# A recommendation tower in blocks of 512 samples: wider lookups, gathers that stand still for the grams, and grams turned straight from PSUM

## The chip, the cores and the metric

The kernel runs on one core of a Trainium2 chip. The time is the device time in microseconds (us) of that core; lower is better. The engines are TensorE (PE in the rows, its weight loads PEld), VectorE (DVE), ScalarE (ACT), GpSimd (POOL) and SyncE (SP), which issues DMAs. Each runs its own instruction stream in order, and they wait for each other by semaphores. One changed kernel is compared with one kernel before.

## The reference: what is computed

For each of 2048 samples there is a dense row of 128 numbers and 26 table ids. Each id picks one row of 128 numbers from its table (tables have 1000 to 125000 rows). The 27 vectors are multiplied with each other, and the upper triangle of products goes, with the dense row, into a small network:

```python
e = jnp.stack([tbl_0[ids[:, 0]], ..., tbl_25[ids[:, 25]]], axis=1)      # (2048, 26, 128)
combined = jnp.concatenate([dense_features[:, None, :], e], axis=1)     # (2048, 27, 128)
interactions = jnp.einsum('bfd,bgd->bfg', combined, combined)
iu, ju = jnp.triu_indices(27, k=1)
z = jnp.concatenate([dense_features, interactions[:, iu, ju]], axis=1)  # 128 + 351
h = jnp.concatenate([z, dense_features], axis=1)                        # 607
h = jnp.maximum(h @ W_top1 + b_top1, 0.0)                               # 512
h = jnp.maximum(h @ W_top2 + b_top2, 0.0)                               # 256
y = h @ W_top3                                                          # (2048, 1)
```

All data are fp32.

## The kernel before, in words

The batch is cut into 16 tiles of 128 samples and 8 blocks of 256. `emb` holds, for two blocks, the 27 vectors of each sample with the 128 numbers across the partitions. It is filled in two ways.

A **look** (`look`, L421 and L422) fetches rows of a table of 1000 rows without a gather. The table lies in SBUF as 8 chunks of 128 rows, each split into a high and a low part (`table_hl`). For a chunk c VectorE compares the ids of the block with the row numbers and writes a one-hot matrix `hot` of 128 x 256 (L646; some are made by ScalarE, L529 and L532). PE multiplies the high and the low part of the chunk with it. 8 chunks, 16 matmuls of 256 columns, add up in PSUM, and ScalarE copies two looks at once into `emb` (L538). Ten tables are looked up in the first six blocks and eleven in the last two. `hot` is a ring of 8: VectorE waits for `hot_used`, which PE raises once for each chunk.

An **embed** (`embed`, L432) handles the other tables. GpSimd gathers 128 rows of one table by an indirect DMA (L391). Three or four such rows blocks, one of them the dense rows of the tile, form a group, and a group fills one of 7 slots of `rows`. PE turns the group by transposes, and ScalarE copies it into `emb`. GpSimd waits for `embeds_done` before it uses a slot again, and for nothing else.

The **gram** of a tile is 128 small products, 26 x 26 each. An fp32 product is two MATMUL records in the trace, so a tile has 256 of them, and they are issued in four bursts of 64, with other work of PE between the bursts (L448). ScalarE copies each half tile to `gram_sb` (L563), VectorE transposes 32 x 32 pieces of that into `turned` (L660), and ScalarE picks the 351 products of a sample into `pairs` (L574 to L581). These are ten small copies for each tile.

The **network** runs on units of two tiles (the last two tiles each alone): `z` transposes the pairs, `l1` is 12 matmuls for each of 4 outputs, `l2` is 12 for each of 2 outputs, `l3` is the last layer. ScalarE and VectorE split each result into a high and a low part.

The order is written by a table of times: each step gets a number from `AT` and formulas around it, and all steps, sorted by it, are the list `STEPS`. Each engine runs its share of `STEPS` in that order. GpSimd alone has its own plain loop over tiles and groups.

Of the kernel before, what the change touches and what calls it, by code (L numbers as in the profile page):

```python
# [7 lines left out]
AT = {"high": 0.1, "low": 0.0, "wload": -0.626, "hots": 0.001, "g0": 0.053, "g1": 0.352, "gs": 0.159,  # L8
# [12 lines left out]
BLOCK_LOOKUPS = [10] * 6 + [11] * 2  # L21
# [8 lines left out]
BLOCK = 256  # L30
# [22 lines left out]
def dlrm_tower(nc, dense, ids_gathered, ids_looked_up, tables, w1_dense, w1_pairs, b1, w2, b2, w3, out):  # L53
# [9 lines left out]
    UNIT_OF = {t + i: u for u, (t, n) in enumerate(UNITS) for i in range(n)}  # L63

# [4 lines left out]
    GROUP = [grouped(list(range(BLOCK_LOOKUPS[t * TILE // BLOCK], FEATURES))) for t in range(TILES)]  # L69
# [6 lines left out]
    BURSTS = 2  # L76
# [7 lines left out]
    ACT_CHUNKS = (3, 7)  # L84
# [7 lines left out]

    def look_time(k, h):
        b, i = LOOKS[k]
        return b - 1 + (i + h / 2) / BLOCK_LOOKUPS[b] + (AT["look"] if b else 0.0)

    def embed_time(t, e):
        return ((AT["e0"], AT["e1"], AT["e2"], AT["e3"])[t] if t < 4 else t / 2 + AT["em"]) + AT["es"] * e / len(GROUP[t]) + (AT["em1"] if t % 2 else 0.0) + (
            AT["em14"] if t == TILES - 2 else AT["em15"] if t == TILES - 1 else 0.0)

    for i in range(LOOKUPS):
        at(-1.6 + 0.1 * i if i >= RAW else -2.0 + i / 100, "load", i)
        at(-1.1 + 0.1 * i - AT["high"] if i >= 2 else -1.5 + i / 100, "high", i)
        at(-1.1 + 0.1 * i + AT["low"] if i >= 2 else -1.35 + 0.05 * i, "low", i)
# [6 lines left out]
    for t in range(TILES):  # L111
# [5 lines left out]
        if t >= TILES - 2:  # L117
            begin = t // 2 + (AT["ug1"] if t % 2 else AT["ug0"])
# [609 lines left out]
```

## Time and profile before

| | |
|---|---|
| three runs | 577.74, 588.22, 592.58 us; median 588.22 |
| span of the profiled execution | 590.3 us |
| PE busy | 437.2 us, 6480 matmuls |
| VectorE, ScalarE, GpSimd busy | 256.1, 200.2, 245.8 us |
| granted TensorE clock, mean | 0.820 |

The profiled execution has no time of its own beside its span of 590.3 us; that lies within the three runs, 0.4% above their median. Busy times overlap and say only how long an engine had something in it. A matmul's record lasts longer than the step from one matmul to the next, since matmuls are pipelined: 256 columns last 0.28 us in the record and follow each other after 0.12 us at the full clock.

### The profile page before, as it was taken

Reading aid. Unit: us, or ns where it says so; the run is one execution under the profiler, and the core shown is the slowest. Engines: PE = TensorE matmul, PEld = TensorE weight load, DVE = VectorE, ACT = ScalarE, POOL = GpSimd, SP = SyncE. Lnnn points to the kernel's source line nnn. Section 1 sums busy time; section 2 is a strip of 40 time slices with the busy share of each in tenths; the row PEclk is TensorE's granted clock in tenths of the full one; section 3 lists DMA queues with packets and bytes.
Section 4 is the critical chain, followed back from the end, with each engine's and each line's share of the span. In section 5 each row is a group of like instructions: output and inputs, shape, how many; then the busy total and the mean of one; then the engine's idle time right before and its main releaser. Section 6 shows DMA issues by size and latency. Waiting matters only on the chain.

```text
span 590.3 us, 15061 instructions
## 1 busy us (share of the span) xinstructions
PE 437.2 (74%) x6480; PEld 394.1 (67%) x6480; DVE 256.1 (43%) x745; ACT 200.2 (34%) x497; POOL 245.8 (42%) x261
## 2 busy tenths in 40 slices
PE   5468266967686866977679594795856879769988
PEld 5267155857576755867558593694755868669987
DVE  4278245742235422455324462352531465537321
ACT  3179122432133311333213341142320333225663
POOL 7705664364425443164431655417344254541000
PEclk9569669977799587888778886787676988879999
DMA  7535211111112111021110211102111111111000
GB/s 264 177 113 162 53 48 45 38 54 37 47 33 55 49 39 41 20 59 42 42 41 25 59 42 48 40 25 62 37 42 44 30 53 43 53 44 29 2 4 1
DMA packets 25781, 31.59 MB, mean 54 GB/s; under 512 B 6469, under 2 KB 19669, under 8 KB 25716
## 3 DMA queue, kind: packets, MB, share of 16 engines
q0 software_dynamic: 8064, 16.53, 9.9%
q1 hardware_dynamic: 17620, 14.10, 8.0%
q8 instruction: 51, 0.84, 0.6%
q14 instruction: 14, 0.11, 0.1%
q10 hardware_dynamic: 32, 0.01, 0.0%
HBM read 30.61 MB, written 0.01 MB: 52 GB/s over the span
## 4 chain that ended last, share of the span: by engine, by line
PE 69%; issue 21%; ACT 5%; another core or an unknown queue 4%; DVE 1%; DVEq 0%; ACTq 0%
PE emb_ps L421 17%; PE emb_ps L422 15%; PE mix_ps L448 13%; PE emb_ps L432 6%; PE mlp_ps L479 4%; PE mlp_ps L480 3%; PE mlp_ps L481 3%; ACT emb L538 2%; PE mlp_ps L490 2%; PE mlp_ps L491 2%; PE mlp_ps L492 2%; PE mlp_ps L509 1%; PE mlp_ps L461 1%; ACT table_hl L516 1%
## 5 line engine op out<-in xcount | busy, mean ns | idle before, releaser
L391 POOL DMA_INDIRECT rows<-table,gather_ids x252 | 244.6, 971 | 298.1 <-PE emb_ps L432 218.4
L646 DVE TENSOR_SCALAR hot<-lids,row_number 128x256 fp32r<-128x256 int16 x638 | 198.7, 365 | 237.0 <-PE emb_ps L422 192.3
L421 PE MATMUL emb_ps<-hot,table_hl 128*128 128x256 f32 x656 | 206.4, 340 | 37.4 <-issue 21.3
L422 PE MATMUL emb_ps<-hot,table_hl 128*128 128x256 f32 x656 | 191.7, 317 | 1.9 <-issue 1.9
L421 PEld LDWEIGHTS emb_ps<-hot,table_hl 128*128 128x128 f32 x656 | 147.2, 224 | 49.2 <-issue 27.9
L422 PEld LDWEIGHTS emb_ps<-hot,table_hl 128*128 128x128 f32 x656 | 149.0, 227 | 2.0 <-issue 2.0
L448 PE MATMUL mix_ps<-emb 128*26 128x26 f32 x4096 | 80.1, 196 | 81.6 <-issue 77.2
L538 ACT ACTIVATE emb<-emb_ps 128x512 f32<-128x512 f32 (+1 forms) x118 | 80.8, 689 | 166.1 <-PE emb_ps L432 59.5
L448 PEld LDWEIGHTS mix_ps<-emb 128*26 128x26 f32 x4096 | 58.3, 108 | 106.9 <-issue 96.3
L432 PE MATMUL emb_ps<-ident,rows 128*128 128x128 f32 x268 | 51.7, 319 | 20.6 <-ACT emb L538 11.7
L563 ACT ACTIVATE gram_sb<-mix_ps 128x416 f32<-128x416 f32 x32 | 29.3, 917 | 83.2 <-PE mix_ps L448 77.6
L432 PEld LDWEIGHTS emb_ps<-ident,rows 128*128 128x128 f32 x268 | 36.8, 163 | 23.2 <-issue 22.6
L479 PE MATMUL mlp_ps<-zh,w1h 128*128 128x256 f32 (+3 forms) x108 | 32.5, 301 | 4.6 <-issue 3.6
L670 DVE TENSOR_TENSOR h1l<-mlp_ps,h1h 128x256 fp32r<-128x256 f32 (+1 forms) x36 | 14.2, 395 | 47.7 <-ACT mlp_ps L599 47.4
L598 ACT ACTIVATE h1h<-mlp_ps,b_sb 128x256 fp32r<-128x256 f32 (+1 forms) x36 | 16.2, 451 | 52.5 <-PE mlp_ps L481 50.1
L480 PE MATMUL mlp_ps<-zh,w1l 128*128 128x256 f32 (+3 forms) x108 | 32.1, 297 | 0.4 <-issue 0.4
L481 PE MATMUL mlp_ps<-zl,w1h 128*128 128x256 f32 (+3 forms) x108 | 32.1, 297 | 0.2 <-issue 0.2
L479 PEld LDWEIGHTS mlp_ps<-zh,w1h 128*128 128x128 f32 (+1 forms) x108 | 22.5, 208 | 5.2 <-issue 4.0
L490 PE MATMUL mlp_ps<-h1h,w2h 128*128 128x256 f32 (+1 forms) x72 | 24.2, 336 | 0.0
L480 PEld LDWEIGHTS mlp_ps<-zh,w1l 128*128 128x128 f32 (+1 forms) x108 | 22.5, 208 | 1.1 <-issue 1.1
L491 PE MATMUL mlp_ps<-h1h,w2l 128*128 128x256 f32 (+1 forms) x72 | 22.9, 319 | 0.0
L492 PE MATMUL mlp_ps<-h1l,w2h 128*128 128x256 f32 (+1 forms) x72 | 22.8, 317 | 0.0
(48 smaller groups left out, 313.9 us busy)
## 6 DMA issues: line engine op xcount, KB each, us to landing
raw<-table SPq DMA_DIRECT2D x11, 512.0 KB
lids<-ids_looked_up SPq DMA_DIRECT2D x82, 64.0 KB
rows<-table,gather_ids POOLq DMA_INDIRECT x252
rows<-dense SPq DMA_DIRECT2D x16, 64.0 KB
w_stage<-w_pairs SPq DMA_DIRECT2D x2, 256.0 KB
w_stage<-w_dense SPq DMA_DIRECT2D x2, 256.0 KB
w_stage<-w SPq DMA_DIRECT2D x1, 512.0 KB
w_stage<-w_pairs SPq DMA_DIRECT2D x1, 190.0 KB
```

Of the source, the lines that this page charges most:

```text
L391: pool.indirect_dma_start(out=rows[:, use % ROW_SLOTS, q, :], out_offset=None, in_=tables[GATHERED[g]], in_offset=bass.IndirectOffsetOnAxi ...
L421: pe.matmul(bank, table_hl[:, i, 0, cols], hot[:, n % HOTS, :], start=(c == 0), stop=False)
L422: pe.matmul(bank, table_hl[:, i, 1, cols], hot[:, n % HOTS, :], start=False, stop=(c == CHUNKS - 1)).then_inc(hot_used, 1)
L432: last = pe.transpose(emb_bank(use)[:, 128 * q:128 * q + 128], rows[:, n % ROW_SLOTS, q, :], ident[:, :])
L448: last = pe.matmul(bank[32 * j:32 * j + SIDE, SIDE * q:SIDE * q + SIDE], emb[:, s, 1:FEATURES], emb[:, s, 0:SIDE], start=True, stop=True)
L479: pe.matmul(bank, w1h[0:k, c, cols], high, start=(c == 3), stop=False)
L480: pe.matmul(bank, w1l[0:k, c, cols], high, start=False, stop=False)
L481: last = pe.matmul(bank, w1h[0:k, c, cols], low, start=False, stop=(c == 2))
L490: pe.matmul(bank, w2h[:, c, cols], h1h[:, c, own(u)], start=(c == 0), stop=False)
L491: pe.matmul(bank, w2l[:, c, cols], h1h[:, c, own(u)], start=False, stop=False)
L538: act.activation(to, bank, ACT.Copy).then_inc(emb_placed, 1)
L646: dve.tensor_scalar(hot[:, n % HOTS, :], lids[:, k % LIDS, :], row_number[:, c:c + 1], None, ALU.is_equal).then_inc(hot_ready, 1)
```

## The change

- Blocks are 512 samples, four of them. `emb` holds one block instead of two.
- A look makes a one-hot matrix of 128 x 512 and 16 matmuls of 512 columns, which fill one PSUM bank; 11 tables are looked up in each block. All one-hot matrices are made by VectorE. The ring `hot` has 6 places, `lids` 2, `rows` 5 slots.
- A tile's 128 grams are issued in one piece, into a pair of banks. Three tiles' grams follow each other, then one embed group, then those of the fourth tile.
- VectorE turns a tile's grams directly from PSUM; the copies by ScalarE to `gram_sb` are gone.
- GpSimd does not start the gathers of a block before the grams of the block before it are done.
- The network takes two of its three banks from the second pair of gram banks. All units have two tiles.
- The raw tables lie where their low parts will be, so that all are loaded at once.
- The table of times is written in new formulas (its numbers are left out below).

```diff
-BLOCK_LOOKUPS = [10] * 6 + [11] * 2
+BLOCK_LOOKUPS = [11] * 4
-BLOCK = 256
+BLOCK = 512
-    UNITS = [(t, 2) for t in range(0, TILES - 2, 2)] + [(TILES - 2, 1), (TILES - 1, 1)]
+    UNITS = [(t, 2) for t in range(0, TILES, 2)]
-    ROW_SLOTS = 7
+    ROW_SLOTS = 5
-    HOTS = 8
-    RAW, LIDS = 6, 4
+    HOTS = 6
+    LIDS = 2
...
-AT = {"high": 0.1, "low": 0.0, "wload": -0.626, "hots": 0.001, "g0": 0.053, "g1": 0.352, "gs": 0.159,
...
+    FIRST, LENGTH, GROUP_TIME = 90.0, 84.0, 5.0
...
-        emb = sb("emb", [128, 2 * BLOCK, FEATURES])
+        emb = sb("emb", [128, BLOCK, FEATURES])
-        mix_ps = banks("mix_ps", 2)
-        mlp_ps = banks("mlp_ps", 3)
+        mix_ps = banks("mix_ps", 2, width=2)
+        mlp_ps = banks("mlp_ps", 1)
...
+                if t % IN_BLOCK == 0:
+
+                    wait(pool, grams_done, t)
                 for e, group in enumerate(GROUP[t]):
                     use = GROUP_NO[t, e]
                     wait(pool, embeds_done, use - ROW_SLOTS + 1)
...
+            def gram(t):
+                b = t // IN_BLOCK
+                pe.wait_ge(emb_placed, max(
+                    [placed["look_out", k] for k in range(len(LOOKS)) if LOOKS[k][0] == b] +
+                    [placed["embed", t, e] for e in range(len(GROUP[t]))]))
+                wait(pe, turn_done, t - 1)
+                if t % 2:
+                    for n in range(mlp_count_before("gram", t))[-3:]:
+                        if n % 3:
+                            wait_mlp_use(pe, n)
+                for side in range(2):
+                    for q in range(HALF):
+                        for j in range(4):
+                            s = t % IN_BLOCK * TILE + 32 * j + HALF * side + q
+                            col = 512 * side + SIDE * q
+                            last = pe.matmul(mix_ps[t % 2][32 * j:32 * j + SIDE, col:col + SIDE],
+                                             emb[:, s, 1:FEATURES], emb[:, s, 0:SIDE], start=True, stop=True)
+                last.then_inc(grams_done, 1)
...
-            def gram(n):
-                t, side = n // 2, n % 2
-                act.wait_ge(grams_done, n + 1)
-                if side == 0:
-                    wait(act, turn_done, t)
-                act.activation(gram_sb[:, :, HALF * side:HALF * side + HALF].rearrange("p r q -> p q r"),
-                               mix_ps[n % 2][:, 0:SIDE * HALF].rearrange("p (q r) -> p q r", r=SIDE), ACT.Copy) \
-                    .then_inc(gram_out, 1)
...
             def turn(t):
-                dve.wait_ge(gram_out, 2 * t + 2)
-                wait(dve, pairs_done, t)
-                dve.transpose(turned[:, :, :].bitcast(u32), gram_sb[:, :, :].bitcast(u32)).then_inc(turn_done, 1)
+                dve.wait_ge(grams_done, t + 1)
+                wait(dve, pairs_done, t - 1)
+                grams = mix_ps[t % 2][:, :].rearrange("p (h x) -> p h x", h=2)[:, :, 0:SIDE * HALF]
+                dve.transpose(turned[:, t % 2, :, :].rearrange("p r (h q) -> p r h q", h=2).bitcast(u32),
+                              grams.rearrange("p h (q r) -> p r h q", r=SIDE).bitcast(u32)).then_inc(turn_done, 1)
```

How the table of times moves the work is seen in the order of PE. Before, around the first tiles' grams (`mix_ps<-emb`; 32 products here are one burst), in which looks (`emb_ps<-hot`) stand between the bursts:

```order
L448 MATMUL mix_ps<-emb 26x26 [waits gram_out,emb_placed]
L448 MATMUL mix_ps<-emb 26x26 x31
L421 MATMUL emb_ps<-hot,table_hl 128x256 [waits hot_ready]
L422 MATMUL emb_ps<-hot,table_hl 128x256
L421 MATMUL emb_ps<-hot,table_hl 128x256 [waits hot_ready]
L422 MATMUL emb_ps<-hot,table_hl 128x256
L421 MATMUL emb_ps<-hot,table_hl 128x256 [waits hot_ready]
L422 MATMUL emb_ps<-hot,table_hl 128x256
L421 MATMUL emb_ps<-hot,table_hl 128x256 [waits hot_ready]
L422 MATMUL emb_ps<-hot,table_hl 128x256
```

In the changed kernel the same place, the end of the first block, has the last embed groups, three tiles' grams, one more embed group, the fourth tile's grams, and then the transposes of the network:

```order
L417 MATMUL emb_ps<-ident,rows 128x128 [waits dense_low,rows_in4]
L417 MATMUL emb_ps<-ident,rows 128x128 x3
L435 MATMUL mix_ps<-emb 26x26 [waits emb_placed]
L435 MATMUL mix_ps<-emb 26x26 x127
L435 MATMUL mix_ps<-emb 26x26 [waits emb_placed]
L435 MATMUL mix_ps<-emb 26x26 x127
L435 MATMUL mix_ps<-emb 26x26 [waits turn_done,emb_placed]
L435 MATMUL mix_ps<-emb 26x26 x127
L417 MATMUL emb_ps<-ident,rows 128x128 [waits emb_placed,dense_in1,rows_in0]
L417 MATMUL emb_ps<-ident,rows 128x128 x3
L435 MATMUL mix_ps<-emb 26x26 [waits turn_done,emb_placed]
L435 MATMUL mix_ps<-emb 26x26 x127
```

No looks stand between the grams any more. On GpSimd the gathers of a block now begin behind a wait for these grams (the first row below); the row before it is the last group of the block before:

```order
L383 DMA rows<-table,gather_ids 128x128 [waits embeds_done]
L383 DMA rows<-table,gather_ids 128x128 x2
L383 DMA rows<-table,gather_ids 128x128 [waits embeds_done,grams_done]
L383 DMA rows<-table,gather_ids 128x128 x3
L383 DMA rows<-table,gather_ids 128x128 [waits embeds_done]
L383 DMA rows<-table,gather_ids 128x128 x3
```

The wait for `grams_done` stands at the first group of each block but the first one.

## Rows read from the trace of the kernel before

**Rows 1.** The page: span, and busy time of each engine.

```profile
span 590.3 us, 15061 instructions
PE 437.2 (74%) x6480; PEld 394.1 (67%) x6480; DVE 256.1 (43%) x745; ACT 200.2 (34%) x497; POOL 245.8 (42%) x261
```

**Rows 2.** The page: the chain of work that ended last, by engine.

```profile
PE 69%; issue 21%; ACT 5%; another core or an unknown queue 4%; DVE 1%; DVEq 0%; ACTq 0%
```

**Rows 3.** Costliest groups: count, busy us, mean ns, idle us before, releaser.

```profile
L391 POOL DMA_INDIRECT rows<-table,gather_ids x252 | 244.6, 971 | 298.1 <-PE emb_ps L432 218.4
L646 DVE TENSOR_SCALAR hot<-lids,row_number 128x256 fp32r<-128x256 int16 x638 | 198.7, 365 | 237.0 <-PE emb_ps L422 192.3
L448 PE MATMUL mix_ps<-emb 128*26 128x26 f32 x4096 | 80.1, 196 | 81.6 <-issue 77.2
L563 ACT ACTIVATE gram_sb<-mix_ps 128x416 f32<-128x416 f32 x32 | 29.3, 917 | 83.2 <-PE mix_ps L448 77.6
```

**Rows 4.** Timeline of PE, a gram burst inside a run of gathers: start, us, count.

```profile
212.61 0.47 PE L448 MATMUL mix_ps<-emb 128*26 128x26 f32 x35
213.48 0.25 PE L448 MATMUL mix_ps<-emb 128*26 128x26 f32 x4 [0.40 <-issue]
...
220.77 0.32 PE L448 MATMUL mix_ps<-emb 128*26 128x26 f32 x6 [0.51 <-issue]
```

**Rows 5.** Timeline of PE at full clock without gathers: a gram burst, then 256-column matmuls.

```profile
564.05 0.73 PE L448 MATMUL mix_ps<-emb 128*26 128x26 f32 x64
564.71 0.39 PE L490 MATMUL mlp_ps<-h1h,w2h 128*128 128x256 f32 x1
...
565.17 0.29 PE L490 MATMUL mlp_ps<-h1h,w2h 128*128 128x256 f32 x1
565.29 0.28 PE L491 MATMUL mlp_ps<-h1h,w2l 128*128 128x256 f32 x1
```

**Rows 6.** Timeline of GpSimd: first and last of nine gathers that follow each other.

```profile
181.92 0.94 POOL L391 DMA_INDIRECT rows<-table,gather_ids  x1 [0.30 <-issue]
...
192.00 0.95 POOL L391 DMA_INDIRECT rows<-table,gather_ids  x1 [0.31 <-issue]
```

**Rows 7.** Stretches: PE, PEld, DVE, ACT, POOL busy (count), PE clock, DMA.

```profile
12.10:31.10 19.00, 6.46 (x20) 4.32 (x20) 4.07 (x9) 2.80 (x5) 14.69 (x15) 0.61 0.56 201
180.70:192.90 12.20, 6.69 (x54) 6.26 (x53) 5.97 (x17) 3.64 (x14) 9.46 (x10) 0.89 0.24 65
```

**Rows 8.** Stretches, same columns: one of nine short gather runs, and their sum.

```profile
131.40:134.90 3.50, 3.50 (x29) 3.50 (x28) 1.80 (x6) 1.66 (x3) 2.84 (x3) 0.89 0.26 65
...
sum 40.00, PE 35.44 PEld 33.73 DVE 26.43 ACT 14.98 POOL 32.81; mean PE 3.94 PEld 3.75 DVE 2.94 ACT 1.66 POOL 3.65
```

**Rows 9.** Timeline, first run of 22 gathers (2.6 to 31.1 us), and just behind it.

```profile
28.36 0.35 DVE L646 TENSOR_SCALAR hot<-lids,row_number 128x256 fp32r<-128x256 int16 x1 [3.12 <-remote]
28.77 0.58 PE L421 MATMUL emb_ps<-hot,table_hl 128*128 128x256 f32 x1 [2.41 <-issue]
31.16 0.35 DVE L646 TENSOR_SCALAR hot<-lids,row_number 128x256 fp32r<-128x256 int16 x1 [2.45 <-issue]
...
38.65 1.66 DVE L646 TENSOR_SCALAR hot<-lids,row_number 128x256 fp32r<-128x256 int16 x6
```

**Rows 10.** Stretches without gathers, columns as in rows 7.

```profile
243.00:253.70 10.70, 10.39 (x277) 9.63 (x278) 5.62 (x20) 4.89 (x17) 0.03 (x1) 1.00 0.08 22
```

**Rows 11.** Stretches, PE and PEld of the grams alone: a long one in the tail.

```profile
557.50:562.20 4.70, 2.38 (x192) 1.95 (x192) 1.00 0.02 3
```

**Rows 12.** Timeline of PE: an embed group of four transposes and what follows it.

```profile
183.09 0.60 PE L432 MATMUL emb_ps<-ident,rows 128*128 128x128 f32 x4
183.44 0.36 PE L421 MATMUL emb_ps<-hot,table_hl 128*128 128x256 f32 x1
```

**Rows 13.** Groups by shape: VectorE's turn and a copy of ScalarE.

```profile
L660 DVE STREAM_TRANSPOSE turned<-gram_sb 128x832 uint32<-128x832 uint32 x16 | 16.5, 1033 | 1.3 <-ACT gram_sb L563 1.3
L538 ACT ACTIVATE emb<-emb_ps 128x512 f32<-128x512 f32 x80 | 59.3, 745 | 105.6 <-PE emb_ps L422 58.6 <-remote 36.1 <-PE emb_ps L432 9.9
```

More of the change, by code:

```diff
@@ new lines, in dlrm_tower @@
+    for b in range(BLOCKS):
+        first = b * IN_BLOCK
+        last_rows = embed_time(first + IN_BLOCK - 1, len(GROUP[first]) - 1)
+        at(last_rows - 4.6, "gram", first)
+        at(last_rows - 2.8, "gram", first + 1)
+        at(last_rows - 0.4, "gram", first + 2)
+        at(last_rows + 0.4, "gram", first + 3)
+        at(last_rows - 2.7, "turn", first)
+        at(last_rows - 0.3, "turn", first + 1)
+        at(last_rows + 1.1, "turn", first + 2)
+        at(last_rows + 1.2, "turn", first + 3)
+        at(last_rows + 1.15, "pairs", first)
+        at(last_rows + 1.25, "pairs", first + 1)
+        after = ends(b)
+        at(after + 2.0, "pairs", first + 2)
+        at(after + 2.1, "pairs", first + 3)
+        u = first // 2
+        if b < BLOCKS - 1:
+            plan = [(0.3, 5.0, 2.5, 19.0, 3.0, 27.0), (29.0, 33.0, 3.0, 47.0, 3.0, 55.0)]
+        else:
+            plan = [(0.3, 2.5, 1.5, 9.2, 1.5, 13.0), (8.8, 12.2, 1.5, 18.5, 1.5, 22.0)]
+        for v, (z_at, l1_at, l1_step, l2_at, l2_step, l3_at) in enumerate(plan):
+            for c in range(2):
+                at(after + z_at + 0.1 * c, "z", u + v, c)
+            for n in range(N1):
+                at(after + l1_at + l1_step * n, "l1", u + v, n)
+            for n in range(N2):
+                at(after + l2_at + l2_step * n, "l2", u + v, n)
+            at(after + l3_at, "l3", u + v)
@@ L142, in dlrm_tower @@
+    for j in range(6):
+        at(58 + 2 * j, "weights", j)
     STEPS = [step for _, _, step in sorted(timed)]
-    def pair_of_looks(k):
-        first = k - LOOKS[k][1] % 2
-        return first, min(first + 1, k - LOOKS[k][1] + len([1 for b, _ in LOOKS if b == LOOKS[k][0]]) - 1)
+    STEP_NO = {step: i for i, step in enumerate(STEPS)}
     emb_bank_of, emb_before = {}, {}
-    last_step = [None] * 3
-    through = [-3, -2, -1]
+    last_step, through = [None] * 3, [-3, -2, -1]
     for now, s in enumerate(STEPS):
-        if s[0] == "embed" or (s[0] == "look" and s[2] == 0 and pair_of_looks(s[1])[0] == s[1]):
+        if s[0] == "embed" or (s[0] == "look" and s[2] == 0):
@@ L162, in dlrm_tower @@
     mlp_use = {s: i for i, s in enumerate(mlp_uses)}
-    placed = {s: i + 1 for i, s in enumerate(s for s in STEPS if s[0] == "embed" or (
-        s[0] == "look" and s[2] == 1 and pair_of_looks(s[1])[1] == s[1]))}
-    over_raw = [s for s in placed if s[1] >= (BLOCK_LOOKUPS[0] if s[0] == "look" else 2)][0]
+    for u in range(2, len(UNITS)):
+        for t in (2 * u, 2 * u + 1):
+            assert STEP_NO["l1", u - 2, N1 - 1] < STEP_NO["embed", t, len(GROUP[t]) - 1]
     ctx = ExitStack()
@@ L270, in run @@
                     parts[what](*n)
-        def by_scalar(n):
-            return CHUNKS <= n < CHUNKS * BLOCK_LOOKUPS[0] and n % CHUNKS in ACT_CHUNKS
-        def hots_by(scalar, n):
-            return sum(by_scalar(m) == scalar for m in range(n))
         def emb_bank(use):
@@ L290, in wait_emb_bank @@
                 what, n, e = before
-                if what == "embed" and e == len(GROUP[n]) - 1:
+                if what == "look":
+                    engine.wait_ge(emb_placed, placed["look_out", n])
+                elif e == len(GROUP[n]) - 1:
                     engine.wait_ge(dense_low, n + 1)
@@ L433, in embed, with mlp_count_before @@
                 last.then_inc(embeds_done, 1)
[L435 to L451 removed]
+            def gram(t):
[16 more added lines that the diff above has]
+                last.then_inc(grams_done, 1)
+            def mlp_count_before(*step):
+                return len([s for s in mlp_uses if STEP_NO[s] < STEP_NO[step]])
             def z(u, c):
@@ L691, in _ @@
             dve.wait_ge(const_ready, 2)
[L692 removed]
+            run({"low": low, "hots": hots, "embed": embed, "turn": turn, "z": z, "l1": l1, "weights": weights})
 def kernel(**inputs):
```

304 lines of the change are left out of this document (114 added, 190 removed), and 5 rows, old and new, of the table AT.

## The prediction

> **What bounds the kernel now.** I read the page first: PE is busy 74% of the span, all other engines under half [rows 1], and the chain that ended last is PE for 69% and "issue" for 21% [rows 2]. So PE sets the time, and in a fifth of it PE has nothing to wait for that the profile shows. Then I looked for where that issue time lies. The grams' group has 80.1 us busy and 81.6 us idle before it, nearly all of it "issue" [rows 3]: 162 us for 4096 matmuls. The timeline shows two kinds of burst. Without gathers 64 of them start within 0.66 us, 10 ns each [rows 5]. With gathers running 35 go through and the rest dribble out in clusters of 1 to 6 every 0.7 us, and the burst takes 8.5 us [rows 4]. Of the 64 bursts, those that overlap a run of gathers are slow, the others are not. At 0.66 us they would cost 64 x 0.66 = 42 us, so gathers cost the grams 162 - 42 = 120 us.
>
> Next, what gathers do to other work. I count PE's work in "warm us", the step of each matmul at the full clock: 256 columns 0.12 [rows 5], a transpose 0.35/4 = 0.09 [rows 12]; the few of 128 columns are taken as 0.12 too. A stretch without gathers has 277 matmuls in 10.7 us, three gram bursts among them, at clock 1.00: PE is full [rows 10]. Nine short runs of 3 to 6 gathers hold 206 matmuls in 40 us (one of them and their sum are in [rows 8]): 5.2 per us, 0.62 warm us per us. Runs of ten hold 54 in 12.2 us, a rate of 0.53 [rows 7]. In the first run, of 22, PE has 20 matmuls in 19 us, a rate of 0.13 [rows 7]; there VectorE and PE each issue one step about every 3 us and then wait again [rows 9]. So a gather run hurts more the longer it lasts. GpSimd itself isn't slowed: nine gathers in 192.00 - 181.92 us, eight steps of 1.25 (one is 1.33) [rows 6].
>
> **The change part by part.** Warm work before: looks 1312 x 0.12 = 157, embeds 268 x 0.09 = 24, the network 648 x 0.12 + 8 for `z` and `l3` = 86, grams 42; sum 309 us. After: looks 704 of 512 columns at 2 x 0.12 = 169 (11 tables instead of 10.25, which costs 11), embeds 256 x 0.09 = 23, network 576 x 0.12 + 8 = 77, grams 42; sum 311. **The change removes no work of PE**; it can only remove waiting.
>
> The span outside the grams' stalls is 590 - 120 = 470 us for 309 warm us: 0.655 per us, clock and waits included.
>
> 1. *Gathers stand still in the grams.* The 120 us go, if PE reaches the grams late enough that GpSimd has nothing of this block left; with the rate above PE needs over 100 us for a block and the 60 gathers need 60 x 1.25 = 75, so it does. At the old rate the rest takes 311/0.655 = 475 us.
> 2. *Gathers bunch elsewhere.* Every block now starts with all 5 slots free: 4+4+4+3+4 = 19 gathers, 23.8 us in a row, four times. By the rates of rows 7, 12.2 us at 0.53 and 11.6 at 0.13 are 8 warm us instead of 15.5: 7.5/0.655 = 11 us lost each, 46 in all. Before has its own such runs in the 0.655 (the first 19 us, 15 us lost; five runs of ten, 2 each): 25. Net +21. Bounds: 0 if 512 columns hide it (the number of steps may be what is slowed, not the columns), +90 if the run is stretched (below).
> 3. *Wide looks.* 161 us are lost beyond warm work outside the stalls. 1312 of 2384 matmuls outside the grams are looks, so some 90 us of it are theirs, and the number of looks' matmuls and of handshakes with VectorE is halved: -45. Bounds 0 (all is the clock) and -90. The one-hot steps of 512 columns take twice 0.26 us on VectorE, 88 x 0.52 = 46 us in a block of some 110 (six of 256 columns in a row last 1.66 us, (1.66 - 0.35)/5 = 0.26 for each step [rows 9]), so VectorE (43% busy now) stays under PE; the ring falls from 8 places to 6 but each is twice as long.
> 4. *One `emb`.* PE can't begin looks of a block before the last grams of the one before. At each end it waits for a copy of ScalarE (0.75 [rows 13]) before the third and the fourth tile's grams and for the turn between: about 3.5 us, four times, +14. Bounds +5 and +30.
> 5. *Turn from PSUM.* Two copies of 0.92 us for each tile go from ScalarE [rows 3], 29 us of an engine that is 34% busy; the turn itself takes 1.03 us [rows 13], from PSUM between that and twice it. It is off PE's path, except in the tail (+-2). 0.
> 6. *Start and tail.* First block: ScalarE's share of the compares goes to VectorE, 18 of them, 18 x 0.35 = 6 us, and stays below PE's time there. Tail: two full units after the last gram, 144 x 0.12 = 17 us plus handshakes, about 25 us; before, two units of one tile, 17 us of matmuls too but partly ahead of the last gram. An estimate: +5; bounds 0 and +15.
>
> Sum: 475 + 21 - 45 + 14 + 5 = **470 us**. I add 15, half of what I left uncosted: the planned order has embeds at fixed places, and rows that come 7 us after the restart can hold PE there (4 x 0 to 8 us). **485 us**, against the profiled 590.3, which lies 0.4% above the median of the runs; I don't correct for that.
>
> On the width of looks, rows give 0.12 us for 256 columns, and nothing for 512. The Trainium skill ("TensorE: Matmul & The Clock Gate", Back-to-back issue gap) has a fixed part of about 2.5 ns beside the columns, some 216 ns for 512. By it the looks are 152 instead of 169, and the sum would be some 20 us lower; no row here shows it, and I don't use it.
>
> **The rivals.**
>
> *A. GpSimd becomes the bound (0.15).* If halving the steps frees PE altogether (rate near 1, as in rows 10), a block takes 60 x 1.25 = 75 plus the restart: the landing, an embed and its copy 1.4, two tiles' grams 5.3, together about 9. Then 9 + 4 x 84 + 25 = 370 to 385 us. For: the warm work of a block, 311/4 = 78, fits into 84. Against: PE would need 0.93 of its time, and in no gather run does it have over 0.62 on average.
>
> *B. Grams in one piece are not 10 ns each (0.17).* All fast bursts are 64 long and stand behind long matmuls. The stretch in the tail has 192 gram matmuls and 8 transposes in 4.7 us with no gathers, and it stalls once: 4.0/192 = 21 ns [rows 11]. Now 256 come in one piece and 768 nearly so. 4096 x 21 = 85 instead of 42, so 485 + 43 = 528 us. The same rival covers a stop that doesn't do what it says: it holds back only the next block's gathers, so if PE is early, the first tiles' grams still meet this block's last ones; a burst that meets a long run costs 8.5 - 0.66 = 7.9 us more [rows 4], and six such are 47 us, the same. The Trainium skill ("TensorE: Matmul & The Clock Gate", "Wait — 56ns, not 53.3ns?") says that starts of small matmuls are never under about 25 ns apart; rows 5 have 10 ns, so the measurement speaks against it as a floor. Taken at its word it would be 102 us for the grams, 545 us in all.
>
> *C. Slower: the opening run feeds itself (0.14).* In a long run PE crawls at 0.13 [rows 7, 9]. Each embed that it does frees a slot, so GpSimd goes on, and the run may last 40 of the 60 gathers: 6 us at 0.53, 44 at 0.13, 25 at 0.62, an average of 0.33 over 75 us. Then 300 us of gathers hold 99 of the 269 warm us outside grams, the rest takes 170/0.655 = 260, and with grams 42, ends 14 and start 9 the time is 625 us. It is over 600 when PE's rate in gather time falls below about 0.38. For: four openings instead of one, and 19 gathers against ten. Against: the crawl's only full example also had the loading of tables beside it, at 201 GB/s [rows 7], and a look step now carries twice the work.
>
> *D. Little gained beyond the grams (0.10):* width saves nothing and the ends cost 30: 545 to 590 us.
>
> **How the numbers follow.** My forecast case (0.44) has 440 to 530 us, the bounds of parts 2 to 4 taken about half way. The range of 8 in 10 leaves out C and about half of A: 392 to 590 us. A difference of under 2% can't be told from none here. Faster by over 2% (below 576 us): forecast case, A, B and most of D, 0.79. Within 2%: 0.07, the end of D and the near edge of C. Slower: 0.14.
>
> **What would show it.** The grams' group should have under 30 us idle before it instead of 81.6, and its bursts 2.6 to 3 us for a tile (10 ns); 5 us for a tile is B. The matmuls of looks should step by 0.22 to 0.24 us at the full clock. GpSimd should have four runs of about 19 gathers; if PE's matmuls in their last 12 us are under 1 per us, part 2 or C holds; if GpSimd's waits for `embeds_done` nearly vanish, it is A. I would be wrong at the root if grams still stalled with GpSimd idle: then it is not the gathers that slow PE.

## The result and the profile after

The changed kernel takes 525.16 us (median of 4 runs, 521.89 to 529.54) against 586.91 us for the kernel before beside it: a ratio of 0.900, interval 0.889 to 0.910. Faster, as forecast (485, range 392 to 590), by 62 us; forecast were 105 (485 against the profiled 590.3). The profiled run took 523.87 us. Each ratio is taken against the kernel before, run again beside the same group of experiments (its medians there were 584.06, 587.58 and 593.30 us), and leaves out runs that took over 1.5% longer than the fastest of their kernel; medians count all runs. Between runs of different groups the ratio is the safer measure, and where the two differ both are given.

The page of the changed kernel: span, busy time, the chain, and the groups that answer to [rows 1 to 3].

```profile
span 521.4 us, 13082 instructions
PE 366.8 (70%) x5788; PEld 306.5 (59%) x5788; DVE 210.1 (40%) x453; ACT 169.9 (33%) x406; POOL 265.1 (51%) x248
...
PE 63%; issue 22%; DVE 4%; ACT 4%; another core or an unknown queue 2%; POOL 2%; DMA 1%; ACTq 0%; SPq 0%; DVEq 0%
...
L383 POOL DMA_INDIRECT rows<-table,gather_ids x240 | 264.1, 1101 | 198.0 <-PE mix_ps L435 90.7
...
L598 DVE TENSOR_SCALAR hot<-lids,row_number 128x512 fp32r<-128x512 int16 x352 | 151.2, 489 | 59.4 <-PE emb_ps L407 26.1
...
L435 PE MATMUL mix_ps<-emb 128*26 128x26 f32 x4096 | 52.2, 214 | 52.4 <-issue 48.7
```

The grams' group fell from 80.1 + 81.6 us [rows 3] to 52.2 + 52.4 = 104.6, so 57 of the profile's 69 us were won there. But I had forecast under 30 us idle before it, and over half of that idle time is still there although GpSimd now stands still. The stretches of the grams, one per block, columns as in [rows 7]:

```profile
94.00:123.20 29.20, 15.48 (x1031) 13.70 (x1031) 3.50 (x5) 3.94 (x23) 0.94 (x1) 0.52 0.04 11
224.50:250.60 26.10, 13.71 (x1030) 12.26 (x1028) 3.46 (x5) 4.24 (x24) 0.00 (x0) 0.69 0.03 8
348.70:374.40 25.70, 13.56 (x1032) 12.23 (x1031) 3.50 (x5) 4.20 (x24) 0.00 (x0) 0.67 0.03 7
467.00:495.50 28.50, 14.27 (x1031) 12.87 (x1030) 3.49 (x5) 4.18 (x24) 0.00 (x0) 0.61 0.02 5
```

One gather falls in the first of them, none in the others, and PE is busy for half. PE's timeline in the second (start, us, count, idle before) shows in what portions:

```profile
231.06 1.71 PE L435 MATMUL mix_ps<-emb 128*26 128x26 f32 x128 [2.25 <-issue]
234.79 1.71 PE L435 MATMUL mix_ps<-emb 128*26 128x26 f32 x128 [2.02 <-issue]
238.11 1.71 PE L435 MATMUL mix_ps<-emb 128*26 128x26 f32 x128 [1.62 <-issue]
```

Exactly 128 matmuls, with their weight loads 256 instructions, then a stop of 1.6 to 2.3 us, one portion every 3.3 to 3.7 us. The DMA queues of the same stretch (packets, MB, share) hold the reason:

```profile
q8 instruction: 8, 0.13, 2.1%
q1 hardware_dynamic: 144, 0.07, 0.9%
```

Eight packets of 0.13/8 MB = 16 KB in 26.1 us, one for each portion. By this PE runs out of instructions; b2 below tests that. The Trainium skill ("Runtime: NRT & Kernel Launch", Instruction fetch mechanics) says that an engine's instructions are refilled in blocks of 16 KiB, 256 of them, and that the cost of this is mostly hidden. The trace agrees on the block; for matmuls as short as these it isn't hidden.

Outside the grams the gathers follow each other in runs, 0.30 us apart. In the first block all 60 are one run (2.8 to 95.0 us). Blocks 2 to 4 open with runs of 27, 23 and 27; here they are whole, and below them a later run of 15, same columns:

```profile
123.30:160.40 37.10, 24.90 (x132) 19.80 (x130) 13.41 (x30) 10.41 (x34) 29.05 (x27) 0.89 0.21 54
250.90:282.20 31.30, 18.48 (x102) 15.75 (x102) 9.51 (x22) 8.77 (x31) 24.60 (x23) 0.83 0.20 55
374.50:409.70 35.20, 21.51 (x108) 17.07 (x106) 11.62 (x26) 10.37 (x34) 27.20 (x27) 0.79 0.21 57
443.40:463.80 20.40, 20.01 (x113) 16.32 (x112) 13.59 (x31) 8.64 (x14) 16.09 (x15) 1.00 0.29 66
```

The opening runs are thin toward their end. These stretches were picked out of the three of them (their last 18, 19 and 14 gathers), and the two below, of four gathers each, out of later runs:

```profile
137.90:160.30 22.40, 10.87 (x45) 7.35 (x43) 3.75 (x8) 2.51 (x4) 17.22 (x18) 0.83 0.21 53
258.50:282.20 23.70, 12.12 (x76) 10.21 (x74) 4.59 (x11) 4.95 (x9) 18.19 (x19) 0.86 0.23 62
392.50:409.70 17.20, 3.93 (x9) 1.85 (x7) 1.76 (x4) 2.66 (x4) 13.22 (x14) 0.67 0.19 53
313.10:317.80 4.70, 4.68 (x32) 4.15 (x31) 0.42 (x1) 1.03 (x3) 3.75 (x4) 1.00 0.26 73
430.00:435.10 5.10, 5.10 (x38) 4.77 (x37) 2.33 (x6) 1.84 (x4) 4.17 (x4) 1.00 0.39 80
```

PE is busy 98% of the later run of 15, 59 to 67% of the opening runs, and 23 to 51% of their thin ends: part 2 of the prediction. The timeline of all engines in the third says what everyone waits for:

```profile
390.24 0.28 PE L470 MATMUL mix_ps<-zl,w1h 95*128 95x256 f32 x1
...
390.37 0.60 PE L417 MATMUL emb_ps<-ident,rows 128*128 128x128 f32 x4
...
399.19 0.47 ACT L553 ACTIVATE h1h<-mix_ps,b_sb 128x256 fp32r<-128x256 f32 x1 [5.19 <-remote]
...
404.12 0.66 ACT L518 ACTIVATE emb<-emb_ps 128x512 f32<-128x512 f32 x1 [4.12 <-remote]
...
406.93 0.54 DVE L598 TENSOR_SCALAR hot<-lids,row_number 128x512 fp32r<-128x512 int16 x1 [5.68 <-remote]
407.52 0.29 PEld L406 LDWEIGHTS emb_ps<-hot,table_hl 128*128 128x128 f32 x1 [5.26 <-issue]
```

PE ends the last `l1` matmul at 390.5 and the transposes at 391.0, each raising a semaphore. ScalarE, idle since 394.0, starts what waits for the first at 399.2 and for the second at 404.1, and the trace has the two raises 9 and 13 us after the work. So work done isn't seen as done for that long.

How often this happens, the semaphore events tell only roughly. Over 0.5 us after the end of the matmul the next event comes for 102 of the 352 raises of `hot_used`, and over 2 us after it for 33; over 2 us also for 18 of the 64 of `embeds_done` and 16 of the 72 of `mlp_full`. But not every raise has an event of its own (274, 54 and 62 have), and in 11 of the 18 cases of `embeds_done` ScalarE had begun its copy before the next event, so the raise had come before it. Where an engine that needs the raise hadn't begun within 2 us either, 22, 7 and 7 at most are left. The 16 of `grams_done`, raised with no gather running, come within 0.03 us.

### The profile page after: what moved, and what is told of

The parts are those of the page before. It is cut to its first block, busy times and chain, and to the rows that moved or that the text cites. A ratio compares the mean times of both kernels' runs of the same rounds, so it can differ in the third digit from the quotient of the medians.

```text
span 521.4 us, 13082 instructions
## 1 busy us (share of the span) xinstructions
PE 366.8 (70%) x5788; PEld 306.5 (59%) x5788; DVE 210.1 (40%) x453; ACT 169.9 (33%) x406; POOL 265.1 (51%) x248
## 3 DMA queue, kind: packets, MB, share of 16 engines
q0 software_dynamic: 7680, 15.74, 11.6%
## 4 chain that ended last, share of the span: by engine, by line
PE 63%; issue 22%; DVE 4%; ACT 4%; another core or an unknown queue 2%; POOL 2%; DMA 1%; ACTq 0%; SPq 0%; DVEq 0%
PE emb_ps L406 16%; PE emb_ps L407 16%; PE mix_ps L435 10%; PE emb_ps L417 6%; PE mix_ps L470 2%; PE mix_ps L468 2%; POOL rows L383 2%; PE mix_ps L469 2%; DVE hot L598 2%; ACT emb L510 1%; ACT emb L518 1%; PE mix_ps L479 1%; PE mlp_ps L479 1%; PE mix_ps L481 1%
## 5 line engine op out<-in xcount | busy, mean ns | idle before, releaser
L383 POOL DMA_INDIRECT rows<-table,gather_ids x240 | 264.1, 1101 | 198.0 <-PE mix_ps L435 90.7
L406 PE MATMUL emb_ps<-hot,table_hl 128*128 128x512 f32 x352 | 152.4, 433 | 74.7 <-issue 39.0
L598 DVE TENSOR_SCALAR hot<-lids,row_number 128x512 fp32r<-128x512 int16 x352 | 151.2, 489 | 59.4 <-PE emb_ps L407 26.1
L407 PE MATMUL emb_ps<-hot,table_hl 128*128 128x512 f32 x352 | 144.8, 411 | 0.0
L406 PEld LDWEIGHTS emb_ps<-hot,table_hl 128*128 128x128 f32 x352 | 70.2, 200 | 101.8 <-issue 50.2
L510 ACT ACTIVATE emb<-emb_ps 128x512 f32<-128x512 f32 x44 | 53.5, 1215 | 113.6 <-PE emb_ps L407 111.6
L435 PE MATMUL mix_ps<-emb 128*26 128x26 f32 x4096 | 52.2, 214 | 52.4 <-issue 48.7
L407 PEld LDWEIGHTS emb_ps<-hot,table_hl 128*128 128x128 f32 x352 | 70.7, 201 | 11.7
L518 ACT ACTIVATE emb<-emb_ps 128x512 f32<-128x512 f32 x64 | 43.4, 687 | 44.8 <-PE emb_ps L417 22.3
L417 PE MATMUL emb_ps<-ident,rows 128*128 128x128 f32 x256 | 45.3, 310 | 17.0 <-DMA rows<-table,gather_ids 14.7
L613 DVE STREAM_TRANSPOSE turned<-mix_ps 128x832 uint32<-128x832 uint32 x16 | 16.8, 1050 | 84.8 <-PE mix_ps L435 80.9
L468 PE MATMUL mix_ps<-zh,w1h 128*128 128x256 f32 (+1 forms) x72 | 20.7, 288 | 0.1
L469 PE MATMUL mix_ps<-zh,w1l 128*128 128x256 f32 (+1 forms) x72 | 20.6, 286 | 0.0
L470 PE MATMUL mix_ps<-zl,w1h 128*128 128x256 f32 (+1 forms) x72 | 20.5, 284 | 0.0
```

The source lines that it names most:

```text
L383: pool.indirect_dma_start(out=rows[:, use % ROW_SLOTS, q, :], out_offset=None, in_=tables[GATHERED[g]], in_offset=bass.IndirectOffsetOnAxi ...
L406: pe.matmul(bank[:, :], table_hl[:, i, 0, cols], hot[:, n % HOTS, :], start=(c == 0), stop=False)
L407: pe.matmul(bank[:, :], table_hl[:, i, 1, cols], hot[:, n % HOTS, :], start=False, stop=(c == CHUNKS - 1)).then_inc(hot_used, 1)
L417: last = pe.transpose(emb_bank(use)[:, 128 * q:128 * q + 128], rows[:, n % ROW_SLOTS, q, :], ident[:, :])
L435: last = pe.matmul(mix_ps[t % 2][32 * j:32 * j + SIDE, col:col + SIDE], emb[:, s, 1:FEATURES], emb[:, s, 0:SIDE], start=True, stop=True)
L468: pe.matmul(bank, w1h[0:k, c, cols], high, start=(c == 3), stop=False)
```

## The experiments

**Two: what the gathers cost at all, and what standing still is worth.**

```
a1_no_stop:   -  if t % IN_BLOCK == 0:
              -      wait(pool, grams_done, t)
a2_plain_dma: -  pool.indirect_dma_start(out=rows[...], in_=tables[...], in_offset=...)
              +  sp.dma_start(rows[:, use % ROW_SLOTS, q, :], tables[...][0:128, :])
```

> GpSimd no longer waits for the block's grams, so gathers run inside them; all else is the changed kernel (525.16 us). In its trace the four gram stretches sum to 109 us with no gather in them, in runs of 128 matmuls (1.3 us) and stops of about 2 us, and GpSimd waits 90.7 us for grams. Theory 1 (what instructions cost to bring in sets the grams, gathers or not): the gram stretches stay at 105 to 125 us, and GpSimd, free 90 us earlier, spreads the opening runs of 19 gathers over the grams: 485 to 515 us. Rival (gathers do slow grams, as in the kernel before, 161.7 us for them): gram stretches 150 to 165 us, what is won elsewhere is at most the 20 us of the opening runs: 545 to 570 us.

> Each gather of GpSimd is replaced by a plain transfer of the same size, rows 0 to 127 of the same table to the same rows of SBUF, issued by SyncE; so the rows that are embedded are other rows, and y is not the reference's. It still stands still during grams. Theory (gathers that GpSimd works out are what freezes the other engines in long runs: 7 matmuls in 12.5 us, 9 in 17.2 us): the freezes go, the stretches without grams (396 us of the span in all) run at about the pace of the quiet stretches, 340 us or less for them, 440 to 475 us in all; gram stretches stay at 105 to 115 us. Rival (it is the data landing in SBUF or the packets on the queues that slow the engines, whoever issues them): 510 to 530 us. Second rival (what the other engines wait for is only rows): the transfers arrive just as late and time stays at 500 to 530 us with waits for rows in their place.

Without the stop: 539.13 us (runs from 532.37 to 543.69; ratio to before 0.917, 0.904 to 0.930). That is 14 more than the changed kernel by the medians and 10 by the ratios, and the intervals overlap, so it isn't clear of noise; it lies between my two cases. Its gram stretches and their sum:

```profile
96.30:147.00 50.70, 18.83 (x1030) 15.77 (x1029) 3.44 (x4) 3.93 (x23) 18.92 (x20) 0.53 0.12 31
226.50:268.00 41.50, 18.36 (x1029) 15.31 (x1028) 3.44 (x4) 4.13 (x24) 13.32 (x15) 0.58 0.11 28
...
484.10:511.20 27.10, 13.98 (x1030) 12.70 (x1029) 3.44 (x4) 4.12 (x24) 0.00 (x0) 0.59 0.02 5
sum 161.10, PE 69.87 PEld 59.50 DVE 13.77 ACT 16.30 POOL 45.53; mean PE 17.47 PEld 14.87 DVE 3.44 ACT 4.07 POOL 11.38
```

15 to 20 gathers add 15 to 22 us to a stretch (41.5 for 26.1, 50.7 for 29.2), so here the rival was right on the grams (150 to 165): gathers do slow them, on top of the arrival of instructions. The sum is 52 us more than in the changed kernel, yet the profiled span only 16: the rest of the span is some 36 us shorter (537.3 - 161.1 against 521.4 - 109.5): fewer gathers stand beside the other work there, and behind the first block no run is longer than 15. The stop is a trade: of the 52 us that it shows in the grams it nets 10 to 14.

What gathers do to a burst of grams isn't the late raises. In the middle of a tile's grams PE waits for no semaphore and raises none. In the second stretch of this run no packet of the instruction queue moves between 227.5 and 242.5 us either, yet PE starts 32 matmuls in 14 us, and 192 at once behind the gathers (the last one ends at 239.1):

```profile
235.12 0.28 PE L432 MATMUL mix_ps<-emb 128*26 128x26 f32 x3 [0.51 <-issue]
237.24 0.30 PE L432 MATMUL mix_ps<-emb 128*26 128x26 f32 x3 [1.84 <-issue]
...
241.47 2.62 PE L432 MATMUL mix_ps<-emb 128*26 128x26 f32 x192 [0.50 <-issue]
```

So gathers hold PE's own issue as well as its raises; whether both have one cause is open.

With plain transfers: 446.04 us (ratio 0.769, 0.761 to 0.778), 79 less, for the same bytes and work, and in more packets (34560 where the gathers take 7680). The gram stretches stay (107.7 us). Outside them (start, three blocks, tail), against 402.9 us for the same five stretches of the changed kernel:

```profile
9.00:89.90 80.90, 57.41 (x261) 44.68 (x262) 54.84 (x113) 34.79 (x45) 0.00 (x0) 0.88 0.50 155
116.50:188.50 72.00, 68.59 (x408) 57.76 (x408) 42.89 (x104) 34.91 (x74) 0.00 (x0) 1.00 0.29 78
...
sum 326.20, PE 287.69 PEld 240.56 DVE 188.47 ACT 152.27 POOL 0.00; mean PE 57.54 PEld 48.11 DVE 37.69 ACT 30.45 POOL 0.00
```

A block takes 72 to 74 us with PE busy 95% of it at a clock of 0.96 to 1.00, where the changed kernel takes 93 to 101. Every raise of `hot_used`, `embeds_done` and `mlp_full` is there within 0.03 us. So it is the gathers that GpSimd works out, not the data landing nor the wait for rows, and they cost 77 of the 403 us outside grams. The edit changes the engine that issues, the kind of transfer and its queue together; which of them counts, no run shows.

**Three: density of gathers, number of semaphore writes.**

```
a3_paced:     +  wait(pool, hot_used, 88 * b + min(int(6.25 * (g - 1)), 80))   # blocks 2 to 4, g > 1
a4_half_incs: -  pe.matmul(... low half ...).then_inc(hot_used, 1)
              +  last = pe.matmul(... low half ...)
              +  if n % 2: last.then_inc(hot_used, 1)
c4_pause:     +  for _ in range(2):                                          # behind each gather
              +      pool.memset(idle[:, :], 0.0).then_inc(paused, 1); pool.wait_ge(paused, pauses)
```

> From the second block on, group g of a block's gathers waits until PE has done 6.25(g-1) of the block's 88 lookup steps (at most 80), so the opening run of 19 gathers is cut in pieces. Theory (long runs of gathers freeze the engines, 45 and 76 and 9 matmuls in 22.4, 23.7 and 17.2 us, where short ones let 7 matmuls a microsecond through): two or three of the freezes of 10 us and more go, 500 to 515 us. Rival (the freeze is per gather, wherever it stands): 520 to 530 us; if the pace makes rows late, up to 560 us.

> PE raises the semaphore hot_used after every second lookup step and not after each, and VectorE and ScalarE wait for it so; VectorE may run one step less ahead at times. Theory (in runs of gathers PE's semaphore writes come through 0.7 or 1.4 us apart and that is what everything waits for): half as many such writes, the lookups in runs of gathers go up to twice as fast, 495 to 510 us. Rival (the writes are only late because PE itself is held up, by its instructions' arrival): 522 to 530 us, or a few us more for the shorter lead.

> The changed kernel with two small memsets of GpSimd after each gather, each waited for, some 0.5 us for both, so a gather comes every 1.75 us or so in place of 1.25; all 240 take 120 us more of GpSimd's time, and 60 gathers fill 105 us in place of 75, more than the 93 to 101 us of a block without grams. Theory (PE's semaphore writes wait behind a gather's work, and pile up only because the next gather follows at once): the long freezes and the updates that come over 2 us late (33, 18 and 16 of them on three semaphores now) are nearly gone, blocks are bound by the gathers, 535 to 560 us. Rival (the lateness is of each gather, not of their density): as many late updates as now, 560 us or more.

Pacing: 520.92 us; half the writes: 520.62 us. Both are 4 to 5 us under the changed kernel, their intervals (0.875 to 0.908 and 0.876 to 0.907) overlap its own, and both miss my theories' 500 to 515 and 495 to 510, so alone neither is shown to pay. The pause costs far more than I expected, 609.05 us (ratio 1.026, 1.016 to 1.036), over the 535 to 560 of its theory:

```profile
L386 POOL DMA_INDIRECT rows<-table,gather_ids x240 | 243.3, 1014 | 170.2 <-POOL idle L391 93.7
...
L391 POOL MEMSET idle<- 128x128 f32 x480 | 128.3, 267 | 14.1
```

A step is 117.5/60 = 1.96 us, not 1.75, so a block is 117 us, all GpSimd's. But events over 2 us late fell from 33, 18 and 16 to 8, 2 and 6, over 0.5 us from 102 to 17 on `hot_used`; with the waiting engines looked at as well, from 22, 7 and 7 to 4, 0 and 0. So the same 240 gathers hold up far fewer raises when they don't follow at once, 0.3 us after the last. Two reservations: PE itself has more time for its work in this run, which no run separates from the pause; and a3, whose pace cuts the opening runs in pieces, has as many late raises as the changed kernel (32, 7 and 12 by the second count). Why a gather holds them up at all, no run shows.

**Two: what holds the grams.** Long matmuls among the short ones, once useless, once useful.

```
b2_long_in_grams: +  for d in range(4):   # ahead of each half tile of grams
                  +      pe.matmul(mix_ps[t % 2][:, 512 * side:512 * side + 512], table_hl[...], table_hl[..., 512:1024])
b1_early_looks:   -  at(last_rows - 4.6, "gram", first) ... (whole tiles)
                  +  at(gram_time(t, side), "gram", t, side)            # half tiles
                  +  return rows_end(b - 1) + 0.15 + 0.1 * (2 * i + h)  # look_time of the next block's first 3
                  +  in look_out: if i < EARLY: wait(act, grams_done, IN_BLOCK * b)
```

> The changed kernel with four added matmuls of 512 columns ahead of each half tile of the grams (128 in all; their result is overwritten). By their length they are 128 x 0.235 = 30 us at full clock and 55 us at half; by number they add 3% to the grams' instructions. Theory (instructions arrive at one block of 256 per 3.4 us, whatever PE does in between): grams as long as now plus 3%, 109 to 120 us, kernel 525 to 537 us. Rival (a gram matmul takes PE itself 25 ns, or the stop follows from what PE does): 139 to 164 us of grams, kernel 555 to 580 us.

> The changed kernel (525.16 us) with the first three lookups of blocks 2 to 4, cut in halves of 8 matmuls of 512 columns, put one by one between the half tiles of the grams of the block before; their copies to emb wait until the grams are done. Theory (the grams are held by the arrival of their instructions: 7 or 8 stops of about 2 us in each stretch of 26 to 29 us, with PE free in them): a half lookup is 8 x 0.235 = 1.9 us at full clock, 3.4 at half, so the 18 of them go into the stops; a gram stretch grows to 28 to 33 us with 6 of them in it, the rest of each block has 11.3 to 20 us less on PE, and the kernel takes 485 to 505 us. Rival (each gram matmul costs PE itself 25 ns): the stretch grows by all of the half lookups, to 38 to 46 us, and the time stays at 520 to 530 us. Second rival (a block outside the grams is bound by GpSimd's 60 gathers of 1.25 us, and its freezes): grams as the theory says, but the gain shows as waits for rows, 510 to 520 us.

The records of the 128 long matmuls add up to 39.5 us, and the gram stretches, with them, sum to 115.4 us, against 109.5:

```profile
223.30:252.20 28.90, 20.43 (x1063) 15.54 (x1061) 3.44 (x4) 4.21 (x24) 0.00 (x0) 1.00 0.02 6
...
sum 115.40, PE 84.81 PEld 64.39 DVE 13.77 ACT 16.07 POOL 0.42; mean PE 21.20 PEld 16.10 DVE 3.44 ACT 4.02 POOL 0.11
```

PE is busy 28 us more in them (84.81 against 57.02), for 6 us more time: the grams are held by the arrival of instructions, not by PE. (Of the kernel's runs two, 530.77 and 534.44 us, lie in the 525 to 537 that I expected and two, 544.37 and 545.16, above it, median 539.41; the profiled one is at 530.77.) The clock in those stretches rose from 0.52 to 0.69 to 0.89 to 1.00, and they didn't get shorter by it, so the clock isn't what holds the grams.

With early looks (b1 also spreads the other lookups of a block wider in the order) the stretches take 31.0, 30.1 and 27.7 us with six half looks in each, in place of 29.2, 26.1 and 25.7:

```profile
221.20:251.30 30.10, 23.65 (x1070) 18.91 (x1069) 11.80 (x24) 4.09 (x23) 0.00 (x0) 0.88 0.07 18
```

So some 40 more matmuls of 512 columns went in for 2 to 4 us a stretch. Yet the kernel won only 8 us by the medians and 12 by the ratios: 516.91 us, ratio 0.879 (0.869 to 0.889). The blocks behind the grams are 91.4, 91.6 and 91.4 us, 21 us over the 70 that PE is busy in each. Each opens with a run of 23 gathers in 29.6 to 29.8 us. Split behind its 13th gather, the first of these runs reads:

```profile
130.10:146.80 16.70, 14.60 (x88) 12.47 (x87) 8.41 (x19) 9.21 (x30) 13.02 (x13) 1.00 0.25 59
146.80:159.70 12.90, 5.31 (x12) 2.67 (x12) 0.97 (x2) 0.67 (x1) 9.76 (x11) 0.63 0.23 61
```

The other two do the same: 87 and 91 matmuls beside the first 13 gathers, 13 and 15 beside the rest. The gathers are about as close in the first part (13 in 16.7 us) as in the second (11 in 12.9), so it isn't the density alone that holds the engines; the hold sets in in the course of a run. The theory was right on the grams; on the total the number is the second rival's, but its sign, waits for rows, is weak: PE waits 15 us for rows in all, and 14.7 in the changed kernel.

**Three: undoing the other parts.**

```
b3_split_looks: -  pe.matmul(bank[:, :], table_hl[:, i, 0, cols], hot[:, n % HOTS, :])   # and the low half
                +  for w in range(2):
                +      for s in (slice(0, 256), slice(256, 512)):
                +          last = pe.matmul(bank[:, s], table_hl[:, i, w, cols], hot[:, n % HOTS, s])
                +  last.then_inc(hot_used, 1)
c3_half_tiles:  +  for s in (slice(0, 256), slice(256, 512)):   # PE: both halves of the table, then the next s
                +      pe.wait_ge(hot_ready, 2 * n + half + 1) ... .then_inc(hot_used, 1)
                +      dve.tensor_scalar(hot[:, n % HOTS, s], lids[:, k % LIDS, s], ...).then_inc(hot_ready, 1)
b4_copy_turn:   +  act.activation(gram_sb[...], mix_ps[t % 2][...], ACT.Copy)   # two for a tile
                +  dve.transpose(turned[...], gram_sb[...])
```

> The changed kernel with each lookup matmul of 512 columns as two of 256, 704 more matmuls, with the same semaphores, hot tiles and copies as now. Theory (the wide lookups' gain is half as many semaphores, hot tiles and handshakes in the gathers' way, not half as many matmuls): 522 to 532 us, 2 to 5 us of it for 1408 more instructions to bring in. Rival (the number of matmuls itself costs): 545 to 570 us.

> The changed kernel with the lookups' width undone alone: 256 columns in a matmul and in a hot tile, a semaphore raised for each on both sides, 704 tiles in place of 352. Splitting the matmuls alone took 537.31 us, 12 more. Theory (most of the gain of wide lookups is half as many handshakes beside the gathers): 555 to 575 us. Rival (what counts is the number of matmuls and their instructions): 535 to 545 us.

> The turn straight from PSUM undone: ScalarE copies each half of a tile's grams to SBUF (32 copies of 0.917 us in the kernel before), VectorE turns them from there (1.033 us there, 1.050 us now). The copy's buffer lies where zh lies, so the first z copy of a block waits for the block's last turn, and the weights' split is 10 us earlier. Theory (the way of the turn is worth nothing, as only the last tile's copies, 1.8 us a block, stand ahead of anything that waits): 523 to 535 us. Rival (two copies and the turn, 2.9 us, hold the PSUM buffer that the grams of the next tile but one need, and each of the 12 later tiles waits): 540 to 560 us. Faster than 520 would say that VectorE's reading of PSUM costs something.

Split matmuls: 537.31 us, ratio 0.917 (0.910 to 0.924), 12 more by the medians and 10 by the ratios, between my two cases. Half tiles too: 549.74 us, 0.930 (0.919 to 0.940), between my two cases as well, another 12 or 8. So wide looks are worth 17 to 25 us, and that is clear of noise for both steps together; each step's interval touches or overlaps that of the next, so the shares of fewer matmuls and of fewer handshakes are only rough. What the split pays for isn't shown either: it brings in 1408 more instructions, 5.5 blocks of 256, but also puts two steps of 0.12 us in place of one of 0.23, an estimated 7 us over 704 of them; and in c3 VectorE's compares take 210.7 us in place of 151.2. The copy ahead of the turn: 533.75 us, 0.913 (0.906 to 0.920), 9 or 8 more, which the theory allowed; its interval overlaps that of the changed kernel, and the edit also moved the weights' split and added a wait before `z`, so what the turn from PSUM brings lies between nothing and these 9.

**Two: together.** c1 is b1 with a4; c2 adds the pace, 4.5 lookup steps for each group of gathers.

> Early lookups between the grams (516.91 us alone) together with one raise of hot_used per two lookup steps (520.62 us alone, from 525.16). Theory (the two gains are of different kinds, stops in grams and late semaphore writes beside gathers, and add): 508 to 515 us. Rival (both take from the same waits, the blocks being held by GpSimd's gathers): 515 to 520 us.

> As the run before it, and from the second block on the third and later groups of gathers of a block wait for PE's lookups, 4.5 steps per group, so that no run of 13 gathers opens the block (in the trace of the early lookups those runs take 16.1, 16.2 and 17.6 us with 36 to 42 matmuls in them, where 5 gathers leave 34 matmuls in 6.3 us). Theory (a long run of gathers freezes the others because PE's semaphore writes fall behind in it): about 8 us less per block of three, 490 to 505 us. Rival (the freeze is made up by any run from 3 gathers on, or the paced rows are late): 508 to 525 us.

Without the pace 517.69 us (510.31 to 520.15): that the halved writes add anything to early looks isn't shown, as the rival said. With it 506.48 us, ratio 0.854 (0.846 to 0.861) to the kernel before, between my two cases and the best of all, and the only gain over the changed kernel besides the early looks (barely, 0.869 to 0.889 against 0.889 to 0.910) whose interval stands clear. Against c1 it is 11 us by the medians and 8 by the runs that a ratio would count (510.31 and 517.26 against 503.63 to 507.52). The opening runs are 15 gathers long in place of 27, 19 and 23. But the profiled executions of the two took the same time, 517.26 and 516.63 us, so no trace shows where the gain lies, and c2's has as many late raises as c1's (38, 31 and 24 events over 2 us late against 31, 28 and 23). My theory gave fewer late writes as the way of the gain, and that isn't borne out; alone, pacing wasn't shown to pay.

## Why the prediction was right and where it was wrong

The sign held, and so did the reading that gathers slow the grams. The largest terms of the sum didn't: the grams in one piece, and what the stop is worth.

- **Part 1, the grams (with part 4).** I priced a gram matmul at 10 ns, from bursts of 64 [rows 5], so 42 us, and 14 for the ends; the stretches took 109.5 us. This is the step that failed most, by 53 us, and it is rival B: 104.6/4096 = 26 ns each, 6.5 us for a tile where I had named 5 as B's sign. My reason for B was the one stop in [rows 11]; I read that row rightly, gave it 0.17, and took the fast bursts as the rule. In the kernel before, each burst stands behind long matmuls, in which, as I read it, the next instructions arrive; in one piece of 256 to 1024 there is nothing for them to arrive behind. The 26 ns are not a floor of PE (b2 puts 28 us of other work of PE into nearly the same time), so the figure agrees with the kernel and its reading as PE's own pace doesn't. The 25 ns that the Trainium skill ("TensorE: Matmul & The Clock Gate", "Wait — 56ns, not 53.3ns?") gives as the least between starts of small matmuls is near this average; inside a portion of this trace 128 start in under 1.7 us, 13 ns each or less.
- **Parts 1 and 2, the stop.** I had -120 for the grams and +21 for bunching, 99 us net. With the stop taken out (a1) the grams lose 52 us, the rest wins 36, and the kernel loses 10 to 14. So most of the gain of 62 us doesn't come from the stop. The width brings 17 to 25, the turn at most 9; together 27 to 48. What the blocks of 512, the grams in one piece and the new order bring of the rest, no run undoes.
- **"It is not the gathers"?** I wrote that I would be wrong at the root if grams stalled with GpSimd idle. They do, and that is half of it: with gathers a stretch is 42 to 51 us, without 26 to 29. Gathers and instruction supply both slow grams, and I had put all of the 120 us on the first.
- **All the rest** I forecast at 485 - 56 = 429 us, and it took 523.9 - 109.5 = 414, so 15 less, the 15 that I had added uncosted. In it errors cancel: wide looks brought 17 to 25 where I had 45. That 525 falls on B's 528 is luck too: B had 21 ns for each matmul and counted the 15 us that weren't needed.
- **Part 2, bunched gathers.** The opening runs came, longer than forecast (27, 23 and 27 gathers for 19), and in their last 12 us PE starts 25, 8 and 6 matmuls, under 1 per us in two of three. The +21 can't be measured by itself; a1 shows what the gathers that the stop holds back cost elsewhere, some 36 us, and c2 against c1 that 8 to 11 come back with the pace.
- **Part 3** was mis-sized: 17 to 25 us, not 45. The step of 512 columns is 0.23 us (391.82 to 392.05 on the timeline), within the 0.22 to 0.24 that I named and above the 0.216 that I set beside it. (That would have been 17 warm us less, 26 us of the sum at 0.655, not "some 20".)
- **Part 5** 0 against at most 9. **Part 6**: the tail behind the last gram is 25.9 us, 20.2 before, so +6 for the tail alone.
- **A** didn't come in time, but half of it is there. Its sign came: GpSimd waits 28 us for PE's transposes, where it waited 218. In the blocks 2 to 4 it works on gathers, with the 0.30 us between them, for some 81 of 93 to 101 us, and in b1 for 78 of 91. It is the next bound: a2 shows that without the hold a block would take 72 to 74 us, below GpSimd's 75. **C** was right on the runs and wrong on their price: the first block's run lasted all 60 gathers, more than the 40 that I had, but PE did 319 matmuls beside it, and beside the later runs of 12 and 15 it ran at nearly full pace.

## What to carry to other kernels

Very short matmuls must stand between long ones: a block of 256 instructions came every 3.3 to 3.7 us here, so anything that issues faster than that stops, and other work put in between is nearly free. Gathers by GpSimd that follow each other without a gap delay PE's semaphores by up to 13 us, so count signals beside them as a cost; moving them out of one stage mostly moves their price. Cutting their runs in pieces paid 8 to 11 us here, only once the stops of the grams were filled, and pauses of 0.7 us behind each cost far more than they gave. A burst's pace measured in one surrounding isn't its pace in another.

## What the runs showed of the hardware

- PE's semaphore raises come up to 9 and 13 us late in a run of gathers (390.5 to 399.2, 391.0 to 404.1), within 0.03 us with plain DMAs in their place, and nearly all on time with gathers 1.96 us apart.
- A burst of small matmuls that waits for nothing is held too: 32 in 14 us beside gathers, 192 at once behind them (a1).
- The hold sets in during a run: in b1 87 to 91 matmuls beside the first 13 gathers, 12 to 15 beside the rest of a run of 23.
- A portion of 128 matmuls with their loads takes about 1.3 to 1.7 us and is followed by a stop of 1.6 to 2.3 us, with 16 KB of instructions brought in for each.
- The mean granted clock in the gram stretches was 0.52 to 0.69 with PE busy half of the time, and 0.89 to 1.00 where 32 long matmuls stood among the 1024 short ones (b2).
- VectorE turns a tile of grams from PSUM in 1050 ns, from SBUF in 1033 [rows 13] and 1045 ns (b4): the source makes hardly a difference.
- A compare of 512 columns takes 489 ns against 365 for 256 [rows 3].
